# Layer 0 of a four-layer transformer: the order of maxima, scores and products with V inside a pair of key tiles

## The reference, cut to what matters

```
q, k, v = x @ w_q, split(x @ w_kv)            # 16 heads of 64
q, k = rope(q), rope(k)                       # on the first 32 of each 64
scores = einsum('bhid,bhjd->bhij', q, k) * 64 ** -0.5
scores = where(causal, scores, lowest)        # tokens see only earlier ones
out = softmax(scores) @ v
return out.reshape(b, n, 1024) @ w_out
```

## Time and profile before

| | |
|---|---|
| median of three runs | 5156.76 us |
| the profiled execution | 5170.1 us, its span 5168.8 us |
| TensorE busy, whole span | 4542.4 us, 88% |
| attention of layer 0 | about 115 to 1130 us of the span |
| attention of layer 3 | about 3700 to 5140 us of the span |

### The profile page before, as it was taken

The page is one execution under the profiler, slowest core; times in us unless marked ns, Lnnn a source line. Parts: engine busy times, 40 slices in busy tenths (PEclk is TensorE's granted clock), DMA queues, the critical chain, the costliest instruction groups (busy, mean ns, idle before and its releaser), DMA issues. The chain is left out here.

```text
span 5168.8 us, 68806 instructions
## 1 busy us (share of the span) xinstructions
PE 4542.4 (88%) x27376; PEld 2215.6 (43%) x27376; DVE 3147.9 (61%) x4176; ACT 2499.2 (48%) x3813; POOL 2318.8 (45%) x1323
## 2 busy tenths in 40 slices
PE   5999999977886777858799999978799999999997
PEld 3444444445654333323322222224455555555554
DVE  4656565636765777752477777843465665565663
ACT  2344444436663555642266666652244444445443
POOL 0455555558771577870100000000066666666675
PEclk8999999989997999979799999988799999999998
DMA  1000000011110000000000000000000000000000
GB/s 32 3 3 3 3 3 3 3 29 32 37 28 12 2 2 2 1 5 19 3 2 2 1 2 1 1 9 1 10 3 3 3 1 3 3 3 1 3 1 9
DMA packets 61954, 36.81 MB, mean 7 GB/s; under 512 B 36308, under 2 KB 53888, under 8 KB 61376
## 3 DMA queue, kind: packets, MB, share of 16 engines
q1 hardware_dynamic: 61632, 32.41, 2.5%
HBM read 22.03 MB, written 1.05 MB: 4 GB/s over the span
## 5 line engine op out<-in xcount | busy, mean ns | idle before, releaser
L795 DVE TENSOR_REDUCE L_part<-banks 128x2 f32<-128x1024 f32 (+2 forms) x1600 | 1881.5, 1189 | 965.7 <-PE banks L646 825.0
L780 ACT ACTIVATE L_weights<-banks 128x1024 f32<-128x1024 f32 (+1 forms) x1600 | 1581.1, 1001 | 1056.4 <-PE banks L678 816.1
L704 PE MATMUL banks<-L_weights,L_V 128*32 128x512 f32 (+3 forms) x6400 | 1490.3, 602 | 3.6 <-ACT L_raw L729 1.8
L1002 POOL TENSOR_TENSOR L_wsum<-L_wsum,L_weights 128x1024 f32<-128x1024 f32 (+1 forms) x448 | 995.0, 2221 | 55.8 <-ACT L_weights L780 3.0
L985 POOL TENSOR_TENSOR L_wsum<-L_wsum,L_two 128x1024 f32<-128x1024 f32 x240 | 571.0, 2379 | 841.6 <-DVE L_two L969 838.5
L704 PEld LDWEIGHTS banks<-L_weights,L_V 128*64 128x64 f32 (+1 forms) x6400 | 282.3, 122 | 453.5 <-issue 397.0
L678 PE MATMUL banks<-L_QH,L_KH 64*128 64x512 f32 (+3 forms) x1664 | 432.0, 453 | 17.9 <-issue 10.2
L2513 POOL MEMSET F_xr<- 128x16 f32 x1 | 0.1, 127 | 933.4 <-POOLq L97 933.4
L646 PE MATMUL banks<-L_KH,L_QH 64*128 64x512 f32 (+3 forms) x1664 | 372.5, 429 | 31.7 <-ACT L_weights L780 17.5
L678 PE MATMUL banks<-L_QL,L_KH 64*128 64x512 f32 (+3 forms) x1664 | 372.0, 382 | 0.0
L678 PE MATMUL banks<-L_QH,L_KL 64*128 64x512 f32 (+3 forms) x1664 | 371.7, 381 | 0.0
(11 more groups left out here) (446 smaller groups left out, 5911.7 us busy)
## 6 DMA issues: line engine op xcount, KB each, us to landing
F_early<-F_V SPq DMA_DIRECT2D x63, 128.0 KB, 2.3
F_tab<-xpos SPq DMA_DIRECT2D x8, 512.0 KB, 4.4
F_h<-L_ffn_h_w SPq DMA_DIRECT2D x2, 1024.0 KB, 8.0
F_wqkv<-L_ffn_wqkv SPq DMA_DIRECT2D x2, 768.0 KB
L_cos<-rope_cos SPq DMA_DIRECT2D x1, 1024.0 KB, 5.0
L_sin<-rope_sin SPq DMA_DIRECT2D x1, 1024.0 KB, 7.0
out<-X SPq DMA_DIRECT2D x1, 1024.0 KB, 5.1
F_z<-F_x SPq DMA_DIRECT2D x32, 31.8 KB
```

The costliest lines, as they stand in the source:

```text
L704: mm = pe.e.matmul(O[r, c:BANK], self.V[g % 2][:, kt, h, :], self.W[x % self.NW][:, y, c:BANK], start=kt < starts, stop=kt >= tiles - starts)
L780: act.e.activation(self.W[x % self.NW][:, :, c:BANK], self.banks(it)[:, :, c:BANK], ACT.Exp, scale=self.scale).then_inc(self.exped, 1)
L795: dve.e.tensor_reduce(self.part[n % 3][:, pr, j, p, :], self.banks(it)[:, :, 0:wide], AX.X, ALU.max).then_inc(self.mx_read, 1)
L1002: pool.e.tensor_tensor(acc[:, :, c:BANK], acc[:, :, c:BANK], W[:, :, c:BANK], ALU.add).then_inc(self.summed, 1)
```

## The change

Layer 0 leaves the `APART` branch and takes the other one, with a new switch that puts the second half of the maxima ahead of the second score.

```diff
     APART = False
+    MIRRORED = False
...
             else:
                 items += one + ps[:half] + carried + turns + eager(ys[:-1]) + [("values", x), ("values", x + 1)]
-                items += mid + eager(ys[-1:]) + two + ps[half:]
+                items += mid + eager(ys[-1:]) + (ps[half:] + two if self.MIRRORED else two + ps[half:])
...
 class RotaryAttention(WideAttention):
-    APART = True
+    MIRRORED = True
```

## The result

| | before | after |
|---|---|---|
| median | 5156.76 us (5153.18 to 5168.81, 9) | 5173.65 us (5161.82 to 5174.81, 9) |
| ratio | | 1.0024, 95% interval 1.0013 to 1.0035 |
| profiled execution, its span | 5170.1, 5168.8 us | 5173.3, 5172.0 us |
| attention of layer 0, barrier to barrier | 1063.5 us | 1071.0 us |
| one run of 80 steps (steps 92 to 171) | 256.2 us | 258.7 us |

The changed kernel is slower by a quarter of a per cent; 5136 us, faster, was forecast. Between the profiled executions layer 0 is 7.5 us longer, but the whole only 3.2: a later stage whose code is the same took 661.3 us before and 657.7 after, and from kernel to kernel it varies from 657.7 to 665.5. So I take the size of the effect from layer 0; 7.5 us are 0.15%, inside the interval of the ratio.

A forecast was written before the change was run, and what follows sets the result against it. TensorE was taken as the bound (93% busy in layer 0). Terms summed to -5.0 us per 80-step run, -20 for four, -20.5 with tail and opening: 5156.76 to 5136 us, own range 5122 to 5149, wider range 5104 to 5167.

The forecast's parts named there:

- the price of a round: Layer 0, TensorE: each change from score-like work to products with V and back costs 0.35 us.
- plain pairs: Pairs without rope projection in them or last in the pair before, or adjacent bank-7 items: 24 x 0.35 = -8.4 us per run.
- two waits: Second score's wait for the first's exponential behind divisions, 0.69 us, and 0.31 two pairs later, would go: -1.0 per run.
- the waits themselves: New TensorE waits: 1.85 us twice and 4.2 in steps 92 to 99, 1.9 behind a rope projection last in a pair.
- The single ropes: Pairs with one rope projection last, twice per run with maxima behind: new wait 1.9, old 0.94 gone; +0.5 us.
- the shifts: Shift directly ahead of a projection or denominator, twice: +0.6 us per run; shift, projection and denominator in a row: +1.1.
- Crowded pairs: Layer 0 stretches with many bank-7 items, VectorE the bound: +2.3 us per run at steps 92 to 99, -0.3 at 132 to 137.
- The cluster: Steps 92 to 99, four pairs with 4, 3, 3, 3 bank-7 items: 1.3 us later plus 1.0 for clock, +2.3 per run.
- the spot: Steps 132 to 137, ropes in three pairs, its 2.77 us wait and slow stretch already there: -0.3 us per run.
- the wait of 4.2: TensorE idle between two projections in the second pair of steps 92 to 99; should bring one more low-clock stretch, counted 1.0 us.
- the 2.77: Wait already in the old kernel at steps 132 to 137, followed by a low-clock stretch costing about 1.7 us where TensorE bounds.
- The third rival: Bank 7 in a row decides: low-clock stretches and slipping maxima at steps 92 to 99 cost +10 per run, 5167 us; chance 0.16.

The follow-up runs named there:

- the four kernels with fillers: Discarded extra matmuls put in TensorE's waits: on the changed kernel (1.0023; more of them 0.9986) and on two mixed-order kernels (0.9948; the last, order chosen pair by pair, 0.9917).
- That pair too: Changed kernel, but pairs with several rope projections, a shift plus two bank-7 items, or three carried subtractions (steps 96, 97) keep the old order: 5142.59 us, ratio 0.9964.

## Why the prediction was wrong

**Right: the price of a round, a little high.** 24 plain pairs lost 8.2 us, where 8.4 and another 1.0 for two waits were forecast; the products are groups of eight at 1.86 to 1.87. The two pairs with those waits (steps 162 and 164) are 0.69 and 0.52 shorter and the waits are gone; the other 22 lost 7.0 us, 0.32 each in the mean for 0.35, single ones from +0.06 to -0.91. The Trainium skill, "TensorEngine Tiling (Array Packing)" (Key Properties), says that changing the tiling mode drains TensorE, and gives no price; the trace agrees with about 0.32 us for a round of two changes.

**Right: the waits themselves.** 1.63 and 1.79 for 1.85, 3.91 for 4.2, 1.75 for 1.9; the first maximum of the third pair waits 1.13 for 2.1. The single ropes came out 0.8 below the forecast, the shifts 1.6 above it in all (+3.3 for +1.7). The clock has no part in the latter, as the window over all three shifts shows:

```profile
600.00:682.00 82.00, 77.13 (x589) 45.00 (x591) 47.43 (x69) 36.92 (x71) 47.07 (x33) 1.00 0.02 4
```

There the waits behind a shift's copy are 0.69 three times and that of the denominator for rope 1.38, as counted; small ones for reductions and exponentials (0.17, 0.30 and 0.49 us), which the forecast did not have, come with them.

**Wrong: "Crowded pairs".** The cluster cost +5.8 for +2.3, and the spot +2.2 for -0.3. Six of the 7.6 us between forecast and run are here. Two sentences of this step failed. The first counted one more low stretch, behind the wait of 4.2, priced at 1.0, because it took the 2.77 for the least wait that has one behind it. The runs show two waits of 1.6 to 1.8 us close together doing the same, and two low stretches in every cluster: 3.2 us of the cluster and 2.0 of the spot go away when the waits are filled. The trace of before already spoke against the sentence, in its fourth run, where no wait of 2.77 stands. Timeline of TensorE and a window of the kernel before:

```profile
944.02 0.82 PE L714 MATMUL banks<-L_Wo,L_raw 64*128 64x128 f32 x5 [1.68 <-DVE L_turned L1104]
...
947.04 1.97 PE L704 MATMUL banks<-L_weights,L_V 128*64 128x512 f32 x4
```

```profile
945.80:949.20 3.40, 3.40 (x11) 1.03 (x8) 2.48 (x3) 3.03 (x7) 1.28 (x1) 0.50 0.00 0
```

Behind waits of 0.86, 0.44 and 1.68 us the clock is at the lower level there, in the cluster. The same three waits in the cluster of the three runs ahead of it have no low stretch behind them, so such a place can go either way; I had read one run and taken it for all. The second said that VectorE bounds the stretch and hides TensorE's loss. VectorE does have 36.41 us of work in 47.83, but at the lower clock TensorE brings maxima late and VectorE stands idle, 2.04 and 0.83 us in the rows above. The spot was laid out with durations of the upper clock, though its slow stretch was already in the trace; in the changed kernel its waits are 2.02 and 3.04 us (0.88 and 2.77 before), and the lower clock stands behind both.

**The third rival** named this mechanism, with +10 per run for the cluster. Its sign came in, two low stretches in each cluster, and so did its outcome, slower. Its price did not: the cluster alone is +5.8, under the 7.3 from which it was to decide, and only with the spot (+8.0 together) and the shifts is the gain of the plain pairs gone. I gave it 0.16. What spoke against it ("waits of 1.31 and 1.42 us a few microseconds apart leave the clock up today") was no guide: between those two waits stand a projection and a product with V, 2.1 us of work; in the new order a projection alone, 1.1.

**What stays open.** Which wait a low stretch follows once several are filled: of the four kernels with fillers only the last came out as expected, with a low stretch less in each run and none left. And how much of the 2.6 us that stay in the cluster is waits, how much the fillers.

## What to carry to other kernels

Price a change of TensorE's tiling by distances between starts: it hides in busy time, and here collecting products of one shape was worth about 0.32 us a round where nothing else waits. Do not put items that share a single PSUM bank in a row when a loaded engine empties it; look at their seams first, since here four such pairs (steps 92, 94, 134 and 136) and three shifts ate what 24 plain pairs gave. Read every repeat of a plan in the trace before taking one for all. Lay the crowded pairs out with two lengths for each instruction, upper and lower clock, and choose the order pair by pair instead of for the layer.

## What the runs showed of the hardware that was not expected

**A stage of layer 3 has two lengths.** Windows with the columns of the earlier trace rows, of the kernel before and of "That pair too", ahead of layer 3's attention, where their code is the same:

```profile
3612.60:3670.20 57.60, 54.57 (x192) 29.40 (x192) 8.30 (x32) 14.04 (x19) 0.00 (x0) 0.76 0.00 1
```

```profile
3591.50:3636.50 45.00, 41.99 (x192) 23.84 (x192) 8.30 (x32) 14.03 (x19) 0.00 (x0) 1.00 0.00 1
```

The same 192 matmuls take 57.6 us at a granted clock of 0.76, or 45.0 at 1.00. Of the twelve profiles of this study eight have the long form, in old and new orders alike, and four the short, all of them kernels that mix the orders, so 12.6 us of any two executions' difference can come from here; medians of few runs carry it. The profiled executions of the kernel before and of the changed one have the long form and times of the upper group, and the groups lie about as far apart. That the lower groups have the short form fits, but no profile of them shows it.

**A subtraction under GpSimd's adds.** VectorE's "low" on two inputs in SBUF takes 0.68 us, but not beside an add of GpSimd. Timeline of the kernel before:

```profile
447.98 5.42 POOL L1002 TENSOR_TENSOR L_wsum<-L_wsum,L_weights 128x1024 f32<-128x1024 f32 x2
...
449.44 4.50 DVE L1123 TENSOR_TENSOR L_KL<-L_st,L_KH 128x512 fp32r<-128x512 f32 x2
```

Two of them take 4.50 us for 1.28. Over layer 0 of the kernel before, 52 subtractions that no add overlaps take 0.68 us in the middle and 0.69 at most, and 12 that one overlaps 0.72 to 2.85. The Trainium skill, "GPSIMD Engine Reference" (Key points), says that GpSimd shares its SBUF interfaces with VectorE and contends with VectorE instructions that have two SBUF inputs; the trace agrees, and reductions from PSUM keep their 1.21 to 1.23 us beside the same adds.
